# An audio tower on one core: zeros for TensorE in the prologue, and another order of its first products

## The reference

```
dx = x[:, 1:] - x[:, :-1]
e = [v]; e.append(outer(e[-1], v) / (k + 1))
new[k] = levels[k] + e[k] + sum_i outer(levels[i], e[k - 1 - i])
v = W @ u; v = v / norm(v); u2 = W.T @ v; ...; sig = v @ W @ u2
```

## Time and profile before

| | us |
|---|---|
| median of three runs | 650.7 |
| the profiled execution | 652.26 |
| its span, first to last instruction | 650.3 |
| PE busy | 633.1 (97%) |
| PEld busy | 531.2 (82%) |
| VectorE busy | 405.8 (62%) |
| GpSimd busy | 321.2 (49%) |
| ScalarE busy | 304.1 (47%) |
| mean granted clock of TensorE | 0.997 |

### The profile page before, as it was taken

The page is one execution under the profiler, slowest core; times in us unless marked ns, Lnnn a source line. Parts: engine busy times, 40 slices in busy tenths (PEclk is TensorE's granted clock), DMA queues, the critical chain, the costliest instruction groups (busy, mean ns, idle before and its releaser), DMA issues.

```text
span 650.3 us, 14315 instructions
## 1 busy us (share of the span) xinstructions
PE 633.1 (97%) x4237; PEld 531.2 (82%) x4239; DVE 405.8 (62%) x1033; ACT 304.1 (47%) x719; POOL 321.2 (49%) x336
## 2 busy tenths in 40 slices
PE   5979999999999999999999999999989999999998
PEld 3867888887888888788888778877769999999997
DVE  7876666666666665666666666777565455455540
ACT  3325444455454455444455544444573534443433
POOL 2355544455554455454445454444875315555551
PEclk9999999999999999999999999999999999999999
DMA  8521343343543343343343334111255623333232
GB/s 302 219 97 34 90 105 81 94 115 83 113 109 86 85 117 89 81 100 94 81 109 102 81 91 104 38 37 41 65 143 176 193 54 44 47 47 44 43 38 66
DMA packets 72262, 60.77 MB, mean 93 GB/s; under 512 B 6832, under 2 KB 60976, under 8 KB 71856
## 3 DMA queue, kind: packets, MB, share of 16 engines
q1 hardware_dynamic: 65600, 56.26, 31.9%
q0 software_dynamic: 6640, 4.22, 4.7%
HBM read 17.31 MB, written 26.82 MB: 68 GB/s over the span
## 4 chain that ended last, share of the span: by engine, by line
issue 32%; PE 31%; POOL 27%; DVE 6%; POOLq 2%; ACT 1%; DMA 0%; SPq 0%; ACTq 0%; DVEq 0%
PE bank L1292 29%; POOL z L497 6%; POOL e3l L492 5%; POOL g L486 4%; POOL e L479 4%; POOL z L499 3%; POOL rstd L506 3%; PE bank L1635 1%; DVE z L955 1%; POOL z L501 1%; POOLq L479 1%; PE bank L1471 0%; POOLq L505 0%; DVE ident_b L1128 0%; DMA h<-x_prev 0%
## 5 line engine op out<-in xcount | busy, mean ns | idle before, releaser
L1292 PE MATMUL bank<-whigh,uth 128*128 128x512 f32 x512 | 170.0, 412 | 1.2 <-DVE lowt L849 1.2
L1292 PEld LDWEIGHTS bank<-whigh,uth 128*128 128x128 f32 x512 | 89.6, 189 | 25.9 <-issue 7.4
L1292 PE MATMUL bank<-whigh,utl 128*128 128x512 f32 x256 | 101.2, 395 | 0.0
L585 POOL DMA_INDIRECT out<-prob,ids x39 | 60.9, 1561 | 66.8 <-ACT prob L803 66.8
L497 POOL TENSOR_TENSOR z<-z 128x512 f32<-128x512 f32 x32 | 42.6, 1332 | 100.4 <-DVE z L955 100.4
L506 POOL TENSOR_TENSOR rstd<-rstd,powers 128x1 f32<-128x1 f32 x64 | 35.2, 551 | 101.7 <-DVE rstd L942 55.0
L1292 PE MATMUL bank<-xvo,x 128*128 128x128 f32 x624 | 76.3, 275 | 0.0
L1292 PEld LDWEIGHTS bank<-xvo,x 128*128 128x128 f32 x624 | 72.8, 192 | 0.2 <-issue 0.2
L955 DVE TENSOR_TENSOR z<-bank,v 128x512 f32<-128x512 f32 x64 | 44.2, 691 | 31.6 <-PE bank L1292 27.8
L1292 PE MATMUL bank<-xT,qkw 128*128 128x128 f32 x512 | 62.5, 275 | 0.0
L1292 PEld LDWEIGHTS bank<-xT,qkw 128*128 128x128 f32 x512 | 59.8, 192 | 0.4 <-ACT xT L619 0.3
(11 more groups left out here) (231 smaller groups left out, 1351.8 us busy)
## 6 DMA issues: line engine op xcount, KB each, us to landing
sorted_rows<-blank SPq DMA_DIRECT2D x24, 709.5 KB, 5.5
xvp<-xvo SPq DMA_DIRECT2D x128, 128.0 KB, 2.3
w<-w_t SPq DMA_DIRECT2D x1, 4096.0 KB, 12.1
xvo<-sorted_rows SPq DMA_DIRECT2D x39, 64.5 KB, 1.8
out<-h SPq DMA_DIRECT2D x9, 256.0 KB, 3.3
w<-w_high SPq DMA_DIRECT2D x4, 512.0 KB, 6.4
x_columns<-x2t SPq DMA_DIRECT2D x32, 64.0 KB, 1.6
xg_in<-x_columns SPq DMA_DIRECT2D x8, 256.0 KB, 4.9
```

The lines of the kernel that those rows point to most:

```text
L585: nc.gpsimd.indirect_dma_start(out=out[:, :], out_offset=bass.IndirectOffsetOnAxis(ap=ids[:, j:j + 1], axis=0), in_=y[:, 2 if j == SORTED ...
L1292: return T.matmul(out_, lhsT, rhs, start=start, stop=stop)
```

## The change

A function `busy(n)` is added: n fp32 products of a 128x128 piece of `zeros` with 64 of its columns, into bank 0. TensorE issues 12 of them before it waits for the first product's inputs, and 9 between that product and `sum_level2(0)`. `zeros` is written first in VectorE's queue and has a semaphore. `gram_qkv()` moves from behind `features(0)` to ahead of `sum_level3(0)`. The high and low products of tile 0's features with the high weights, which alternated, come as 8 high ones for both halves, then 8 low ones. On VectorE `signature_lo(0)` goes behind `features_lo(0)`; on ScalarE `signature_hi(3)` goes ahead of `level3_hi(1)`.

```diff
+        zeros_set = sem("zeros_set")
...
             features_hi(0)
+            signature_hi(3)
             level3_hi(1)
-            signature_hi(3)
...
+            V.memset(zeros[:], 0.0).then_inc(zeros_set, 1)
             V.memset(low[:, :, 0:1], 1.0)
-            V.memset(zeros[:], 0.0)
...
             level2(2)
             level2(3)
-            signature_lo(0)
...
             features_lo(0)
+            signature_lo(0)
             d.wait_ge(ld_sn, 48)
             d.wait_ge(norm_mm, 1)
...
+            def busy(n):
+
+                for _ in range(n):
+                    mm(B[0][:, 0:LEN], zeros[:, 0:P], zeros[:, 0:LEN])
+
+            pe.wait_ge(zeros_set, 1)
+            busy(12)
             pe.wait_ge(ld_before, 16)
             pe.wait_ge(small, 1)
...
             def project_first_hi(half_):
 
                 pe.wait_ge(u4_hi, 2)
-                pe.wait_ge(u4_lo, 3)
                 for c in range(UC):
                     pe.wait_ge(w_hi, c + 1)
                     mm(B[1 + half_][:], uth[:, c, :], whigh[:, 0, c, col(half_, 512)], c == 0, False)
+
+            def project_first_mid(half_):
+
+                pe.wait_ge(u4_lo, 3)
+                for c in range(UC):
                     mm(B[1 + half_][:], utl[:, c, :], whigh[:, 0, c, col(half_, 512)], False, False)
...
+            busy(9)
             sum_level2(0)
             pe.wait_ge(ld_w, 16)
             weight_products(B[6:8], PAIRS, wqkv_sb[:, 0:PAIRS, :])
+            gram_qkv()
             pe.wait_ge(before_cast, 1)
             sum_level3(0)
             pe.wait_ge(ld_sq, 32)
             features(0, False)
-            gram_qkv()
-            project_first_hi(0)
+            for half_ in range(2):
+                project_first_hi(half_)
+            for half_ in range(2):
+                project_first_mid(half_)
             sum_level3(1)
             pe.wait_ge(ld_wo, 16)
             pe.wait_ge(norm_step, PRODUCT_STEP)
             weight_products((B[5], B[4]), 2 * PAIRS, woutT)
-            project_first_hi(1)
```

## The result

| | before | changed |
|---|---|---|
| median | 650.58 (649.23 to 653.05, 4 runs) | 658.11 (657.15 to 659.7, 4 runs) |
| profiled execution, its span | 652.26, 650.3 | 658.06, 656.2 |

Times are in us. The ratio is 1.0117, with an interval of 1.0097 to 1.0138: by it the change makes the kernel 7.6 us slower (7.5 by the two medians). The forecast was 650.3 with a range of 648.2 to 654.6, so the kernel moved the other way and beyond the range. R1 had the direction and most of the mechanism, at half the size.

The account below looks back on a forecast made before the run. The prediction took the prologue's chain of waits, mostly VectorE's, as what the change could move: 1.56 us gained behind level4(0)'s start, 1.10 lost before it, 0.46 faster, so a median of 650.3 us, range 648.2 to 654.6.

Parts of the forecast that it names:

- R1: Rival, prologue: the zeros do not bring TensorE's clock up; 3.6 us slower, 654.3; chance 0.28.
- I take 213 ns a pair there: Zeros before the first product: at the low clock each load-and-matmul pair takes 213 ns, bounds 107 and 213.
- R2: Rival, first zeros: a load does not set the pair's time at the low clock; 648.6; chance 0.12.
- if the clock rises on the way, between 5.4 and 6.2: First row of zeros on TensorE: a clock rise during it would let it end between 5.4 and 6.2 us.
- it costs 0.66 instead of 1.21: First real product on TensorE, behind the zeros: takes 0.66 us instead of 1.21.
- S: Start of level4(0) on VectorE, on which its later work hangs: 12.85 us before, forecast 13.95.
- I took 1.35: Delay of VectorE's L907 from zeros ahead of the first product: between 0.8 and 2.2 us, taken as 1.35.
- I took it as covered by 0.6: Zeros before sum_level2(0): its result at 9.45 us, VectorE wants it at 10.0, so no delay.
- I took -0.25: Gram product ahead of sum_level3(0): VectorE's queue reaches level4(0) at 12.60 + 1.35, without its former 0.25 us wait.
- 1.56 us if S stays: VectorE behind level4(0): no wait for the Gram product, so L1117 starts 5.6 us after S instead of 7.16.
- off the path, with 2.7 us to spare: Reordered high and low products on TensorE: work ends at 26.9 us, VectorE weighs at about 29.6; no gain or cost.
- point of decision: In R1, the loss decides once the Gram product ends later than e3l; wholly slow it costs 5.1 us, not 2.6.

Follow-up runs that it names:

- e7: Changed kernel with zero products of one column in place of 64, counts unchanged; 659.13 us (one execution).
- e3: Changed kernel with zeros of 192 columns, 8 and 6 products in place of 12 and 9; 652.03 us, ratio 1.0027 to the kernel before.
- e5: Changed kernel with zeros of 192 columns, only 4 and 2 products so that they fit; 651.05 us, ratio 1.001 to the kernel before.
- e6: Changed kernel with its zeros of 64 columns, but only 6 and 3 products; 652.26 us, ratio 1.003 to the kernel before.
- e9: Changed kernel without the 9 zero products ahead of sum_level2(0), the first 12 kept; 655.06 us, ratio 1.0077 to the kernel before.
- e4: Changed kernel without zeros and with the Gram product in its old place, other new orders kept; 649.66 us, ratio 0.9996 to the kernel before.
- e8: As e5, with the Gram product split in three pieces: ahead of sum_level3(0), behind it, behind the transposes; 650.74 us, ratio 1.0003.
- e11: e5 with the Gram product in its old place behind the transposes; 650.48 us, ratio 1.0003 to the kernel before.
- e10: e5 plus 6 wide zero products ahead of tile 1's transposes; 649.74 us, ratio 1.0005 to the kernel before.
- e1: Changed kernel without both rows of zeros, new order kept; 652.46 us, ratio 1.0023 to the kernel before.

## Why the prediction was wrong

*"I take 213 ns a pair there"* was right: 24 pairs in 5.18 us, the first product at 6.26 (forecast up to 6.2), and e7 shows that it is the load. So R2 is out. By the rule of the Trainium skill ("TensorE: Matmul & The Clock Gate", "LDWEIGHTS (loading the stationary operand)"), an estimate of 107 ns a load, the zeros would have been out of the way at 3.95; the trace, with 214 ns a pair in e7, does not agree.

*"if the clock rises on the way, between 5.4 and 6.2"* and, after it, "it costs 0.66 instead of 1.21": this is the step that failed. I wrote myself that each pair streams columns for only half of its 213 ns, gave that to R1 with 0.28, and then worked out the forecast as if unbroken instructions were enough. The clock stayed low through both rows of zeros: the first product took 1.17 and sum_level2(0) 2.02, not 0.66 and 1.02. e3 against the changed kernel and e5 against e6 show that the narrow products were at fault: the same time, the same zeros, three times the columns per load, and it rises. That zeros as data, or the place, were at fault is excluded by these.

What followed from it, at S: the first product +2.29 (I took 1.35); the second row of zeros +2.12 (I took it as covered by 0.6; slow, its 18 pairs run from 7.22 to 10.95, while VectorE was ready at 10.9); the Gram product ahead of sum_level3(0) +1.49 (I took -0.25). Sum 5.90, against +1.10 in the forecast and +5.15 in R1. e6 and e9 bear out the parts: without both overruns S is 14.18 in e6, which is +1.33 for the Gram product, and the second row alone is worth 2.25 in e9.

*"1.56 us if S stays"* was mis-sized. From S to L1118 it was 6.54 and not 5.6. signature_lo(0) took 2.08 in its new place and not 1.21. It began at 23.18, just after GpSimd's remainder for tile 1:
```profile
22.88 1.30 POOL L493 TENSOR_TENSOR e3l<-e,e3h 128x512 fp32r<-128x512 f32 x1 [1.53 <-ACT e3h L602]
```
In e3 the same instruction took 2.14 behind the same neighbour. The gain was 0.62, and in e4 and e5 it was 0.64. It was lost to the order of these two instructions and not for good: in e8 and e11 signature_lo(0) began first and took 1.22 and 1.23, GpSimd's took 2.24 and 2.25, and L1118 came 5.90 and 5.91 after S, a gain of 1.25. e8's rows:
```profile
17.38 1.22 DVE L850 TENSOR_TENSOR whigh<-w,whigh 128x1024 fp32r<-128x1024 f32 x1
17.51 2.24 POOL L493 TENSOR_TENSOR e3l<-e,e3h 128x512 fp32r<-128x512 f32 x1 [2.29 <-ACT e3h L602]
```

*"off the path, with 2.7 us to spare"* for TensorE was right in order and missed the price of sparing: TensorE waited 2.00 us, the clock fell, and L964 lost 0.60 more (6.60 after the weighing in place of 6.00). e5 has the same loss (0.66) and e10 takes 0.40 of it away. In e3 and e7 TensorE waited 1.63 and 1.48 there, the clock stayed up, and L964 came 5.99 after the weighing.

*The rival that fitted.* R1 had 654.3. The profiles add 5.90 - 0.62 + 0.60 = 5.88 where R1 had 3.6. Its point of decision, a Gram product that ends later than e3l, was right: e3l was ready at 15.9 (15.19 + 0.69), the Gram product ended at 18.0. Of the 0.75 that R1 was short at S most is a slip in its sum: it lets the weight products end at 14.3, but sum_level2(0) that ends at 12.97 and weight products of 2.08 give about 15.0, and the trace has 14.98. What is left up to 7.5 lies behind the loop, about 1.5 us with the load of xg_in in the chain; neither the forecast nor R1 had a term for it, and its cause stays open.

The spacing of the loop's tiles is unchanged: the 5.9 at L964 stays until the stretch at 487 in before.

## What to carry to other kernels

A filler must be priced like work: it stood in TensorE's queue ahead of the first real product, and for narrow fp32 products the load of the weights set the price (213 ns a pair). In these runs only the wide filler brought TensorE's clock up, so try few loads and wide operands, read the next real product's duration to see whether it worked, and let the filler end before the first real input. Here even the filler that fitted and raised the clock brought nothing that the times show. A reorder that makes TensorE early moves its idle time elsewhere; look at what the clock does there, and whether a moved VectorE step now begins just after a GpSimd one.

## What the runs showed of the hardware

- 64-column fp32 products with a 128x128 load each ran at 207 to 216 ns a pair from 1.1 to 10.9 us and left the clock low; behind 192-column ones it was up by the first or second real product (0.84 and 1.02 in e3, 1.13 in e5). In e10, with e5's prologue, sum_level2(0) took 1.59: the moment differs from execution to execution.
- At a granted clock of 0.50, one-column products with a 128x128 fp32 load took 1.71 for 8 in the changed kernel and in e5. Before, at the high level, they took 0.95, the first row below. So the time of such a load follows the clock.
- Behind a 2.00 us wait of TensorE the clock was low for nearly 7 us in the changed kernel (0.50 in the second fence, 39 to 42.9 us) and in e5. The same place shows it in e1, e6 and e9, whose waits were 2.00 to 2.02. A wait of that length doesn't always do it: before has one of 1.97 at 40.52, the second row, and the granted clock stayed at 1.00.
```profile
32.16 0.95 PE L1292 MATMUL bank<-ucol,woutT 128*128 128x1 f32 x8
40.52 0.38 PE L1292 MATMUL bank<-wu_out,x2t 128*128 128x1 f32 x2 [1.97 <-DVE wu_out L1148]
```
```profile
39.00:42.90 3.90, 3.90 (x13) 3.35 (x13) 1.39 (x6) 0.99 (x3) 2.57 (x4) 0.50 0.62 269
```
- Where VectorE's subtraction of 1024 columns and GpSimd's of 512 overlapped, the one that began later was stretched. VectorE's took 1.22 when it began first (e8) and 2.06 to 2.17 in the nine profiles where it began second; GpSimd's took 1.27 to 1.30 when it began first, and 2.24 when it began second in e8.
